# A selective scan, a mixture of experts and causal attention on one core: the list scheduler that writes every engine's order gets other lengths, delays and shifts

## The reference

```python
xn = layernorm(x)                                   # layer 0
xm, res = split(xn @ in_proj_w.T)                   # 512 + 512 channels
xm = silu(causal_conv(xm, 4 taps) + conv_b)
dt, Bm, Cm = split(xm @ x_proj_w.T)                 # 64, 16, 16
delta = softplus(dt @ dt_proj_w.T + b)
h_t = exp(delta_t * A) * h_(t-1) + delta_t * B_t * u_t     # 512 channels x 16 states, 1024 steps
y = (sum_n h * C + u * D) * silu(res)
m = y @ out_proj_w.T
c = m + gelu(m @ ffn_w1.T + b1) @ ffn_w2.T + b2
x = x + (c - mean(c)) / sqrt(var(c) + eps) + moe(xn)       # moe: gelu(xn @ w1) @ w2, weighted
xn = layernorm(x)                                   # layer 1
attn = softmax(causal(q @ k.T * scale)) @ v         # 16 heads of 16
gated = mean over heads of sigmoid(mem_score * s) * sigmoid(xn @ memg_w + b)
x = x + (attn + gated * (xn @ memv_w + b)) @ out_w + out_b \
      + gelu(xn @ (W1 + scale*m1).T + b1) @ (W2 + scale*m2).T + b2
```

## Time and profile before

| | us |
|---|---|
| three runs | 3900.20, 3903.46, 3905.79 (median 3903.46) |
| the profiled execution, its own time | 3907.57 |
| its span, first to last instruction | 3905.8 |

### The profile page before, as it was taken

How to read it: one execution, slowest core, us unless ns; L and a number is a source line. 1 busy time by engine, 2 the same in 40 slices (tenths; PEclk the granted TensorE clock), 3 DMA queues, 4 the chain that set the end, 5 groups by cost and what they waited for, 6 DMA issues and landing times.

```text
span 3905.8 us, 63544 instructions
## 1 busy us (share of the span) xinstructions
PE 3610.2 (92%) x20512; PEld 2387.7 (61%) x20512; DVE 3178.4 (81%) x6108; ACT 2659.1 (68%) x4049; POOL 2288.1 (59%) x1788
## 2 busy tenths in 40 slices
PE   7999999999999999999798999999999998999998
PEld 3666566655556565656565666666566666656665
DVE  3788999998999999998957687786868778686874
ACT  6877878787787878877534657566575656657565
POOL 4687898898999899999814142332414233241421
PEclk9999999999999999999897999999999999999999
DMA  4345444454544555554522123232322323232220
GB/s 155 126 155 162 154 156 157 161 165 151 163 161 153 159 164 171 162 166 144 184 74 90 52 58 97 72 100 67 99 65 69 93 68 104 67 94 64 73 80 26
DMA packets 253340, 456.88 MB, mean 117 GB/s; under 512 B 26116, under 2 KB 80852, under 8 KB 250196
## 3 DMA queue, kind: packets, MB, share of 16 engines
q1 hardware_dynamic: 253012, 452.82, 37.1%
HBM read 381.07 MB, written 69.21 MB: 115 GB/s over the span
## 4 chain that ended last, share of the span: by engine, by line
PE 46%; DVE 13%; ACT 9%; issue 8%; POOL 1%; DVEq 0%; ACTq 0%; POOLq 0%
PE ps L1495 6%; PE ps L1608 5%; PE ps L1600 5%; PE ps L1476 4%; PE ps L1458 3%; DVE ps L2013 3%; PE ps L1360 3%; PE ps L1410 2%; PE ps L1529 2%; PE ps L1370 2%; DVE ps L2036 2%; ACT L1625 2%; PE ps L1535 2%; ACT h L1625 2%; ACT exps L1625 2%
## 5 line engine op out<-in xcount | busy, mean ns | idle before, releaser
L2270 POOL TENSOR_TENSOR drive<-du,b_wide 128x1024 f32<-128x1024 f32 x512 | 1202.0, 2363 | 204.3 <-DVE held L2013 122.1
L2304 POOL TENSOR_SCALAR_AFFINE_SELECT exps<-exps 128x256 f32<-128x256 f32 x512 | 204.1, 413 | 1000.5 <-ACT exps L1625 1000.0
L1625 ACT ACTIVATE ps<-delta,neg_a 128x512 f32<-128x512 f32 x1024 | 681.7, 685 | 146.2 <-DVE heavy L1991 132.2
L1625 ACT ACTIVATE exps<-ps 128x1024 f32<-128x1024 f32 (+1 forms) x640 | 596.5, 938 | 255.2 <-PE ps L1476 249.2
L2036 DVE CUSTOM_DVE_ANT_0 ps<-ps,later 128x512 f32<-128x512 f32 (+3 forms) x1024 | 474.7, 518 | 90.6 <-PE ps L1458 88.6
L1410 PEld LDWEIGHTS ps<-p_all,heavy 128*128 128x128 f32 x3072 | 361.9, 144 | 246.5 <-DVE heavy L1991 124.8
L1410 PE MATMUL ps<-p_all,heavy 128*128 128x128 f32 x3072 | 439.9, 280 | 76.2 <-DVE heavy L1991 69.2
L1991 DVE TENSOR_TENSOR heavy<-c_wide,ps 128x512 f32<-128x512 f32 x704 | 467.6, 670 | 8.2 <-issue 4.1
L2013 DVE TENSOR_TENSOR_SCAN ps<-ps,carry,drive 128x512 f32<-128x512 f32 x352 | 441.5, 1272 | 32.8 <-ACT ps L1625 32.5
L2013 DVE TENSOR_TENSOR_SCAN ps<-ps,drive 128x512 f32<-128x512 f32 x352 | 420.4, 1214 | 48.3 <-ACT ps L1625 46.0
L2039 DVE TENSOR_REDUCE smax<-ps 128x2 f32<-128x1024 f32 x256 | 312.1, 1220 | 112.0 <-PE ps L1458 109.3
(11 more groups left out here) (211 smaller groups left out, 7158.7 us busy)
## 6 DMA issues: line engine op xcount, KB each, us to landing
b_wide<-bc_dram SPq DMA_DIRECT2D x512, 256.0 KB, 3.4
c_wide<-bc_dram SPq DMA_DIRECT2D x512, 256.0 KB, 3.5
stacks<-parts SPq DMA_DIRECT2D x192, 256.0 KB, 2.5
qs<-stacks SPq DMA_DIRECT2D x128, 192.0 KB
ks<-stacks SPq DMA_DIRECT2D x128, 192.0 KB, 4.3
x_row<-in_x SPq DMA_DIRECT2D x14, 1024.0 KB, 7.9
resid<-mix SPq DMA_DIRECT2D x9, 1024.0 KB, 5.3
x_row<-resid SPq DMA_DIRECT2D x9, 1024.0 KB, 5.4
```

The source lines that it names most:

```text
L1625: return nc.scalar.activation(out_, in_, func, **kw)
L2270: G.tensor_tensor(drive[:, g % DRIVE_SLOTS, :, :], du[:, e, :, :], wide(b_wide[:, g % B_SLOTS, :], MD), ALU.mult).then_inc(driven, 1)
```

## The change

The matmuls, vector operations and transfers are the same in number and shape; the table of numbers in the scheduler, the rule by which it picks, and the place of one square root are not.

- Delays: `LATE` gives 0.2 us after PE, 0.18 after ACT, 0.16 after DVE, 0.12 after POOL (0.06 for all before); `OWN` adds 0.13 us between dependent units of different kinds on ACT or DVE; `TO_POOL` 0.09 us from a scan to POOL.
- Lengths are set anew in both layers, most by a few hundredths of a microsecond, some by more (DVE's gate 1.66 to 1.32, spreads 1.3 to 0.55, `lines` 1.1 to 0.6); transfers land later or earlier in the plan (fetch in layer 1 6.0 to 10.4, stack 2.8 to 4.0, keep 7.0 to 5.5).
- PE's clock in the plan goes by columns fed (`ACTIVE`), no longer by a share of time.
- The pick: `SHIFTS` moves the ticks of whole kinds of units, `PULL` lets the tick count on ACT and POOL, `DRIFT` falls from 0.08 to 0.042, `SHORT` from 0.2 to 0, `STAY` 0.02 is new.
- The square root of tiles 4 to 7 stands in the start, right behind the drain of the first transposes.

All of the kernel's lines move down: what was line n is n + 51 from the scheduler on (scan 2013 -> 2064, weigh 1991 -> 2042).

```diff
+LATE = {"p": 0.2, "a": 0.18, "v": 0.16, "g": 0.12, "s": 0.06}
+TO_POOL = 0.09
+OWN = {"p": 0.0, "a": 0.13, "v": 0.13, "g": 0.04}
...
-    def add(engine, unit, length, tick, *after, late=0.06):
+    def add(engine, unit, length, tick, *after, late=None):
...
-        add("v", ("gate", q), 1.66, at + NS * MD + 0.7, ("p", "add", piece_of(j, e + 1, 0, 0) - 1),
-            ("p", "held", q, POOL_STATES[-1]), ("a", "silu_g", j) if j else None)
+        add("v", ("gate", q), 1.32, at + NS * MD + 0.7, ("p", "add", piece_of(j, e + 1, 0, 0) - 1),
+            ("p", "held", q, POOL_STATES[-1]), ("a", "silu_g", j))
...
-TURN, DRIFT = 0.1, 0.08
-SHORT, RUN = 0.2, 2
+TURN, DRIFT = 0.1, 0.042
+SHORT, RUN, STAY = 0, 2, 0.02
+PULL = {"a": 0.026, "v": 0, "g": 0.009, "s": 0.0}
+SHIFTS = {
+    ("a", 0): {"xt": -27, "yt": 3, "res": 21, "skip": 18, "decay": 2.7, "gelu": 23, "dl": 8.1, "xm": 3.6, "soft": 11,
...
+    ("v", 0): {"scan": 45, "weigh": -77, "guard": 31},
...
-                        key = start + DRIFT * (tasks[name][1] - LAYER1_FROM)
+                        key = start + DRIFT * (tasks[name][1] - LAYER1_FROM) + (STAY if own != mode else 0.0)
...
+                else:
+                    key = start + PULL[e] * tasks[name][1]
...
-            felt = end + (late if one[0] != e or e == "s" else 0.0)
+            felt = end + (late if one[0] != e or e == "s" else OWN[e] if kind_of(one) != kind_of(name) else 0.0)
+            felt += TO_POOL if name[:2] == ("v", "scan") and one[0] == "g" else 0.0
...
+    for name, (length, tick, after, wait) in tasks.items():
+        tasks[name] = (length, tick + shift_of(name), after, wait)
...
-                    if (j, task[2]) == (0, TC):
-                        task_of(("root", 0, 1))
...
+                elif unit == ("xt", 0, 0, KD - 1):
+                    task_of(("root", 0, 1))
```

170 lines of the change are left out of this document (97 added, 73 removed), and 6 rows, old and new, of the table SHIFTS.

## The result

| | before | after |
|---|---|---|
| median of four runs | 3903.9 | 3745.9 (3741.8 to 3749.8) |
| profiled execution, its span | 3905.8 | 3740.1 |
| first scan | 61.3 | 59.2 |
| last gate of layer 0 | 1961.1 | 1892.0 |
| scan phase, from the one to the other | 1899.8 | 1832.8 |

The ratio is 0.9596, 95% interval 0.958 to 0.9613. The scan phase gave 67 us (29 forecast) and layer 1 97 us (33 forecast).

A forecast was written before the change was run, and what follows sets the result against it. Taken as bounds: DVE and PE, both nearly full, with DVE waiting for ACT, in the scan phase; PE in layer 1. 3907.6 - 2.7 - 29 - 10 - 30 + 7 = 3843, or 3839 us beside the median; range 3800 to 3870.

The forecast's parts named there:

- The start: Before the first scan: with the square root taken earlier, that scan moves from 61.3 to 58.6 us, a gain of 2.7 us.
- The scan phase: Layer 0: DVE's counted shortfalls at ACT's long blocks fall from 66 to 27 us; with a cut for PE, -29 us.
- the part of the 116 us that the count doesn't explain (50 us): Layer 0: of DVE's 116 us idle hanging on ACT, 50 us lie outside the counted shortfalls and were forecast to stay.
- the cut for PE: First 200 steps of layer 0: only 12 of 22 us counted gain taken, as PE has 12.2 us idle there.
- The joins of POOL: Scan phase: a scan could come to wait for POOL's drive; taken as 0, bounds -5 and +5 us.
- Three output units: Three units of PE move from behind the last scan into the end of the scan phase, where PE idles; -10 us.
- Waits of PE: Layer 1: a bit over a fifth of PE's 139 us idle time goes, -30 us; bounds 0 and -70.
- Layout changes: Layer 1: 80 more changes of PE's layout at 0.09 us each cost 7 us; 25 us at 0.31 us each.
- rival A: Slower by finer interleave in layer 1: 80 changes, each with a wait, cost 68 us; 3930 us, chance 10%.
- Rival C: All waits follow the delays: -55 us in the scan phase, -60 in layer 1; 3783 us, chance 10%.
- B: PE holds layer 0 back to -12 us and layer 1's waits gain nothing; 3891 us, chance 15%.
- D: Gains are taken back where the scan phase meets layer 1, nothing changes; 3896 to 3911 us, chance 6%.

The follow-up runs named there:

- e4: The kernel before with only the square root of tiles 4 to 7 moved to the start, behind the drain of the first transposes; 3903.3 us.
- e1: The changed kernel without the shifts and the pull of ticks; fitted delays, lengths, clock model and pick stay; 3929.9 us.
- e8: The changed kernel with layer 0's shifts of ACT and POOL taken out; 3793.4 us.
- e9: The changed kernel with layer 0's shifts of PE, DVE and the transfers taken out; 3819.3 us.
- e6: The changed kernel with the delay after every engine back at 0.06 us, OWN and TO_POOL as changed; 3905.7 us.
- e13: The changed kernel with the pick's price of leaving a layout of PE at 0.2 us instead of 0.02; 3880.8 us.
- e3: The changed kernel with PE's pick in layer 1 as before (DRIFT 0.08, SHORT 0.2, STAY 0); 3848.4 us.
- e10: The changed kernel planned with the old model of PE's clock, shares of time instead of columns fed; 3793.1 us.
- e2: The changed kernel with all delays set back (LATE 0.06, OWN and TO_POOL 0), shifts kept; 3908.3 us.
- e7: The changed kernel with one shift taken out, that of DVE's guard of the layer norm (seven short instructions); 3759.9 us.
- e5: The changed kernel with only OWN, the delay between dependent units of one engine, set to 0; 3912.7 us.

## Why the prediction was wrong

Direction and places were right: only waits went, no engine lost work, and the likeliest case pointed to faster. Both large terms were too small. By the steps:

*The start,* -2.7: -2.1 measured, -1.6 with the root alone (e4). Right in kind, a little too large.

*The scan phase,* -29: -67 measured. The count of shortfalls at ACT's long blocks said 27 us for the kernel after, and the trace has 19.4 + 6.8 = 26 us named as waits for ACT. The step that failed is "the part of the 116 us that the count doesn't explain (50 us) I leave as it is". I reasoned that the order at these gelus has the same shape. It has, but the table load comes 5.5 us earlier against the steps (3.9 us behind step 640 for 9.4), so DVE has eight pieces in hand where it had three. These waits were counted at single places; which part of the change moved them stays open (e1 leaves 2.0 of the 5.40 us, e8 0.31 and e9 nothing at step 646). Of the 50 us 8 are left: the waits for ACT went from 116 to 34, by 82. About 12 us of new waits (for heavy's ring and for PE at `mix`) are set against it. The second failed step is the cut for PE. In the first 200 steps I took 12 of the 22 counted, and 17.7 were had (407.9 to 390.2 us), although PE is busy 98% there now (335.8 of 341 us). From the first scan to that of step 200 PE's idle time fell from 14.4 to 5.8 us and its busy time by 9.1 us, of which the low clock makes 6 (11.5 us low before, none after). A PE that is 96% busy gave more than its idle time, because part of its busy time was time at 1.2 GHz.

*The joins of POOL,* 0: right; waits for a drive behind the first scan are some 11 us, 9 before.

*Three output units,* -10: the 50 matmuls fewer in layer 1 (12,350 to 12,300) are these, 3 x 3.6 = 11 us of PE's busy time. Right.

*Waits of PE,* -30: -57 measured. "A wait of 0.54 us is longer than that error, so it goes only where another unit now stands in front" is the failed sentence, with the fifth that I took from it: the group of the earlier trace rows went from 21.7 to 3.9 us. e6 shows that delays of 0.06 bring it back with all the shifts in place, e13 that a changed pick does so too. A small error in the plan's numbers changes the whole order, and the order decides these waits.

*A term that was missing:* the clock. I read PEclk in the rows and used it for the last 60 us of layer 0 alone. In layer 1 the time at 1.2 GHz fell from 116 to 66 us, worth 25 us. With the units' 11 it makes 36 of the 40 us by which PE's busy time fell; 4 are left unexplained. e3 and e10 show the mechanism with larger sizes. I also put the scan phase down to waits alone, where 90 us at 1.2 GHz became 33.

*Layout changes,* +7: no cost that shows, by e13, and rival A's 25 us and more with it. The busy time at full clock is 1730 to 1735 us in eight kernels with 12,300 matmuls and between 1191 and 1411 changes. In e2 it is 1748; why is open.

The reading of the earlier trace rows was in part wrong. Its last row is two matmuls side by side, each with 512 columns where the MLP's have 256, so 0.50 for 0.28 us is mostly the width. In the kernel before a 64x512 matmul has a record of 0.49 us behind the whole array and of 0.39 behind its own layout (medians at full clock), and it starts 0.214 us behind the MLP's last for 0.125 inside the MLP. So a change does cost something at its place, 0.09 to 0.10 us. Over 188 of them that would be 17 us, and e13 shows none of it.

The Trainium skill's page "TensorEngine Tiling (Array Packing)", Key Properties, has a change of mode drain the engine. The records behind a change agree that the first matmul takes longer, by that 0.10 us; the kernel with fewer changes isn't shorter for it.

*Sum:* -2 - 67 - 11 - 57 - 25 - 4 = -166, as the spans differ (3905.8 to 3740.1).

Rival C came nearest in kind: waits follow the delays, "the room on PE" was no bar. It was still 37 us too high, for want of the clock and of half the unexplained waits. B and D stood on PE being full, but its own busy time in the scan phase fell from 1768 to 1743 us.

What the experiments say of the change as such: each part taken out alone costs 14 (e7) to 184 us (e1), and four of them (e1, e2, e5, e6) nearly all of the gain or more. I had priced the parts by places in one trace, as if they added up. They don't: a table of shifts is worth its time under the model that it was found with (e2, e5 and e6 for the changed table).

## What to carry to other kernels

Where a planner writes the order, first correct its model by the trace, above all for what it holds to be free, and only then search: a random search of like length made this kernel 79 us slower under the old model and 79 faster under the new one. Count PE's short waits twice where the granted clock falls behind them, and look at PEclk in every stretch before you price idle time. When a count explains only part of the waits, ask how each of the others could go before you leave them standing.
